# Relative attention in a six-layer decoder kernel: a finished batch's normalisation and store placed one step later, behind the step's writes to DRAM

## The chip, the cores and the metric

The kernel runs on one core of one Trainium2 chip. Five engines take part, each with an instruction stream of its own: PE (TensorE, matrix products), DVE (VectorE), ACT (ScalarE), POOL (GpSimd) and SP (SyncE, which here only issues DMAs). They meet through semaphores. The metric is the device time of one execution in microseconds, as the median of several runs; lower is better. The profile is one execution of its own, with its own time.

## The reference

The program is a decoder of two layers with three parts each. After each part comes a residual sum and a layer norm: `x = layernorm(x + part(x))`. The input x is 8 batches x 256 tokens x 256 channels in float32. The parts are retention, cross attention, channel mix, relative attention, an mLSTM cell and a product-key expert layer. The change touches only the fourth, relative attention (16 heads of 16 channels, distances clipped at 64):

```
dist  = clip(idx[None, :] - idx[:, None], -R, R) + R
score = einsum('bhqd,bhkd->bhqk', q, k) + einsum('bhqd,qkd->bhqk', q, rel_emb_k[dist])
attn  = softmax(score)
ctx   = einsum('bhqk,bhkd->bhqd', attn, v) + einsum('bhqk,qkd->bhqd', attn, rel_emb_v[dist])
x     = layernorm(x + ctx @ W_out + b_out)
```

The terms in `rel_emb_k[dist]` and `rel_emb_v[dist]` need each row of a 256 x 256 table shifted by its own row number.

## The kernel before, in words

The whole program is one launch. The six parts are software pipelines that overlap at their seams. Relative attention (`relative_attention_layer`) runs from about 615 us to about 1058 us of the span. Its first steps run beside the last of the channel mix, and from its step 18 on the opening of the mLSTM runs beside it.

The work is cut into units. A unit U is a group of four heads of one batch, so a batch b is units 4b to 4b+3 and there are 32 units. `STEPS` runs s from -5 to 38; in step s every engine handles several units at different stages: the table of query times distance embedding of unit s+3, the scores and exponentials of unit s+1, the turning of the probabilities of unit s, the turning of the skewed probabilities of unit s-2, the values of unit s-3. A finished batch b passes its last stages at fixed steps: PE gathers it at step 4b+7, turns it at 4b+8, and multiplies by the output weights at 4b+9. At step 4b+10 (`out_of(s - 1) == b`):

- DVE adds the residual into `yout` and takes mean and variance (L1670, L131 to L136), before the step's additions of bias (L1630);
- POOL raises the variance to -1/2 (L1532, `rel_rs`);
- DVE, later in the same step, behind its copy of the turned skewed probabilities (L1688) and before its copies of the step's table (L1697), waits for `rstd`, normalises `yout` in place (L141, two instructions) and counts up `y_ready`;
- SP waits for `y_ready`, stores `yout` to DRAM (L1474), and for b = 0 and 1 also loads the input of batch b+6 (L1306, through `take_x`).

The skewing goes through DRAM. SP's step, in its order, is: two loads that read the table back with a skewed pitch, the bias (L1458, after its save has landed); two skewed loads of the probabilities (L1470, after their save has landed); the store and input load above; the save of the table of unit s+3 (L1484, 1 MB, after ACT's and DVE's copies); the save of the probabilities of unit s+1 (L1491, 1 MB, after ACT's exponentials). Each engine takes its stream in order, and so does SP: an instruction that waits holds all behind it.

From step 21 to 28 the mLSTM's steps are chained behind these on two queues. On SP: a load of `mls_v_in` for value batch k+1 (L2032, 256 KB), a wait until POOL has centred batch k, and its store to `mls_v_rows` (L2046). On POOL, from step 20 on: wait for value batch k, then centre it (L2091 to L2099). POOL takes that work behind its own relative-attention step, so the `rel_rs` of the next step comes after it. At step 30 the mLSTM's loads of the finished batches 0 to 4 follow (L1886, each waiting until the batch is stored), and at step 31 the loads of the context, with that of batch 5 behind the first.

```
if (b := out_of(s - 1)) is not None:              # SP, between the loads and the saves
    sp.wait_ge(y_ready, b + 1)
    sp.dma_start(batch_of(x_out, b), yout[:, b % 2]).then_inc(stored[b % 2], 16)
    if b + XS < nb:
        sp.wait_ge(x_used, b + 1)
        take_x(sp, b + XS)
```

Of the kernel before, what the change touches and what calls it, by code (L numbers as in the profile page):

```python
# [51 lines left out]
def batch_of(ap, n):  # L52

    return ap[bass.ds(n, 1)].rearrange("a (t p) d -> p (a t) d", p=P)


def load_all(engine, sem, pairs):

    for to, what in pairs:
        engine.dma_start(to, what).then_inc(sem, 16)  # L60
    return 16 * len(pairs)
# [60 lines left out]
def place(h):  # L122

    g, r = h // 4, h % 4
    return g // 2, g % 2, ROWS * r
# [1205 lines left out]
def relative_attention_layer(nc, mem, bank, ident, room, yout, two_before, before, x_out, w, nb):  # L1331
# [4 lines left out]
    def sem(name):  # L1336
        return nc.alloc_semaphore("rel_" + name)
# [11 lines left out]
    XS = 6  # L1349
# [24 lines left out]
    x_loaded, stored = [sem(f"x_loaded{k}") for k in range(XS)], [sem(f"stored{k}") for k in range(2)]  # L1374
# [11 lines left out]
    x_used, var, rstd, y_ready = sem("x_used"), sem("var"), sem("rstd"), sem("y_ready")  # L1386
# [7 lines left out]
    def unit(k):  # L1394
        return k if 0 <= k < UNITS else None

    def batch(k):
        return k // GROUPS if k % GROUPS == 0 and 0 <= k // GROUPS < nb else None

    def scores_of(s):  # L1400
        return unit(s + 1)

    def table_of(s):
        return unit(s + 3)

    def turn_of(s):
        return unit(s)
# [10 lines left out]
    def project_of(s):  # L1418
        return batch(s + 4)
# [7 lines left out]
    def out_of(s):  # L1427
        return batch(s - 9)

    def head(U, r):  # L1430
        return (U // GROUPS,) + place(4 * (U % GROUPS) + r)

# [4 lines left out]
    def take_x(sp, b):  # L1437
        before["give_x"](sp, b, xin[:, b % XS], x_loaded[b % XS])

    def sync(sp):  # L1440
        load_all(sp, loaded, loads)
        sp.dma_start(wv[:], w["wv"]).then_inc(wv_loaded, 16)
        load_all(sp, late, late_loads)
        yield
        two_before["work_taken"](sp)
        take_x(sp, 0)
        yield
        for s in STEPS:
            if 1 <= s + 6 < XS:
                take_x(sp, s + 6)  # L1450
            if (U := unit(s + 2)) is not None:

                sp.wait_ge(qr_saved[U % 2], 16 * (U // 2 + 1))
                if U >= 2:
                    sp.wait_ge(summed_ready, 4 * (U - 1))
                for t, first in ((0, 2 * (P - 1)), (1, 2 * (2 * P + REACH - 2))):
                    skewed = bass.AP(qr_rows[U % 2].tensor, first, [[2 * PW - 2, P], [PW, 2], [1, 2 * NEAR]])
                    sp.dma_start(bias[:, U % 2, t, :, REACH * t:REACH * t + NEAR]  # L1458
                                 .rearrange("p h k e -> p h (k e)"), skewed).then_inc(bias_loaded[U % 2], 16)
            if (U := turn_of(s)) is not None:  # L1460
                if U == 0:
                    before["over"](sp)
                    before["kept"](sp)

                sp.wait_ge(p_saved[U % 2], 16 * (U // 2 + 1))
                if U >= 3:
                    sp.wait_ge(wT_mm, 2 * (U - 2))
                for t, first in ((0, 2 * NEAR), (1, 0)):
                    skewed = bass.AP(p_rows[U % 2].tensor, first, [[2 * PW + 2, P], [PW, 2], [1, 2 * NEAR]])
                    sp.dma_start(by_dist[:, U % 3, t, :, 0:NEAR].rearrange("p h k e -> p h (k e)"), skewed)\  # L1470
                        .then_inc(dist_loaded[U % 3], 16)
            if (b := out_of(s - 1)) is not None:
                sp.wait_ge(y_ready, b + 1)
                sp.dma_start(batch_of(x_out, b), yout[:, b % 2]).then_inc(stored[b % 2], 16)  # L1474
                if b + XS < nb:
                    sp.wait_ge(x_used, b + 1)
                    take_x(sp, b + XS)
            if (U := table_of(s)) is not None:

                sp.wait_ge(qr_act, 2 * (U + 1))  # L1480
                sp.wait_ge(qr_dve, 2 * (U + 1))
                if U >= 2:
                    sp.wait_ge(bias_loaded[U % 2], 32 * (U // 2))
                sp.dma_start(qr_rows[U % 2], qr[:, U % 2].rearrange("p h k e -> p h (k e)"))\  # L1484
                    .then_inc(qr_saved[U % 2], 16)
            if (U := scores_of(s)) is not None:

                sp.wait_ge(probs_ready, 4 * (U + 1))
                if U >= 2:
                    sp.wait_ge(dist_loaded[(U - 2) % 3], 32 * ((U - 2) // 3 + 1))  # L1490
                sp.dma_start(p_rows[U % 2], probs[:, U % 2, :, REACH:REACH + ROW]  # L1491
                             .rearrange("p h k e -> p h (k e)")).then_inc(p_saved[U % 2], 16)
            yield s


# [123 lines left out]
    def vector(dve):  # L1619
# [27 lines left out]
        for s in STEPS:  # L1647
            if (b := project_of(s - 1)) is not None:
                dve.wait_ge(v_mm, b + 1)
                if b >= 3:  # L1650
                    dve.wait_ge(values_mm, GROUPS * (b - 2))
                dve.tensor_copy(v[:, b % 3, :, :, 0:HD].rearrange("p t h e -> p (t h) e"),
                                bank[2][:].rearrange("p (a e) -> p a e", e=HD)).then_inc(v_ready, 1)
            if (b := gather_of(s - 1)) is not None:
                dve.wait_ge(oU_turned, b + 1)
                if b >= 2:
                    dve.wait_ge(o_turned, b - 1)
                for t in range(TT):
                    parts = bank[1 + t][:].rearrange("p (h e) -> p h e", e=VW)
                    dve.reciprocal(rsum[:, t], parts[:, :, HD])  # L1660
                    dve.drain()
                    last = dve.tensor_tensor(o[:, b % 2, t].rearrange("p (h e) -> p h e", e=HD),
                                             parts[:, :, 0:HD], over(rsum[:, t], HD), ALU.mult)
                last.then_inc(o_ready, 1)
            if (b := out_of(s - 1)) is not None:
                dve.wait_ge(o_mm, b + 1)
                dve.wait_ge(xbo_ready, b + 1)
                if b >= 2:
                    dve.wait_ge(stored[b % 2], 16 * (b // 2))
                dve.tensor_tensor(yout[:, b % 2], tiles(bank[0]), xin[:, b % XS], ALU.add).then_inc(x_used, 1)  # L1670
                dve.drain()
                row_stats(dve, yout[:, b % 2], st[:, b % 2], mv[:, b % 2], ve[:, b % 2]).then_inc(var, 1)
            if (U := turn_of(s - 1)) is not None:
                keep_turned(U, 3)
            if (U := scores_of(s)) is not None:
                add_bias(U, 0)
            if (U := turn_of(s)) is not None:
                keep_turned(U, 1)
            if (U := scores_of(s)) is not None:
                add_bias(U, 1)  # L1680
                add_bias(U, 2)
            if (U := scores_of(s)) is not None:
                add_bias(U, 3)
            if (U := dist_of(s)) is not None:
                dve.wait_ge(wT_mm, 2 * U + 1)
                if U >= 2:
                    dve.wait_ge(values_mm, U - 1)
                dve.tensor_copy(wT[:, U % 2, 0].rearrange("p r s -> p (r s)"), bank[6][:]).then_inc(wT_dve, 1)  # L1688
            if (b := out_of(s - 1)) is not None:
                dve.wait_ge(rstd, b + 1)  # L1690
                normalise(dve, yout[:, b % 2], yout[:, b % 2], mv[:, b % 2], rs[:, b % 2])[-1].then_inc(y_ready, 1)
            if (U := table_of(s)) is not None:
                if U >= 2:
                    dve.wait_ge(qr_saved[U % 2], 16 * (U // 2))
                for r in range(2, 4):
                    dve.wait_ge(qr_mm, 4 * U + r + 1)
                    dve.tensor_copy(table_cut(U, r), bank[r][:, 0:2 * BAND]  # L1697
                                    .rearrange("p (t k) -> p t k", t=TT)).then_inc(qr_dve, 1)
            if (U := unit(s - 1)) is not None:
                far_sums(U)  # L1700
            if x_turn_of(s) == 0:
                dve.wait_ge(late, 16 * len(late_loads))
                dve.wait_ge(const_mm, 1)
                dve.tensor_tensor(const_row[:], tiles(bank[3]), bo[:].unsqueeze(1).broadcast_to([P, TT, D]),
                                  ALU.add).then_inc(const_ready, 1)
            yield s
# [1638 lines left out]
```

## Time and profile before

| what | value |
|---|---|
| median of 3 runs | 1798.02 us (1796.23 to 1798.17) |
| profiled execution: its own time, span | 1808.23 us, 1806.5 us |
| PE busy, share of the span | 1618.8 us, 90% |
| DVE, ACT, POOL busy | 65%, 37%, 18% |
| mean granted TensorE clock | 0.946 |
| chain that ended last | PE 60%, issue 14%, DVE 10%, ACT 4%, DMA 4%, POOL 3% |
| DMA, whole span | 97 GB/s |
| DMA in relative attention | 328, 315, 321, 321, 336, 322, 331, 303 GB/s in 8 of 40 slices |

The page divides the span into 40 slices of about 45 us. In 32 of them the DMA engines are idle or lightly used; in those of relative attention they are 90% busy or more. "Idle before" names the time for which an engine had nothing to run ahead of an instruction and what ended it.

### The profile page before, as it was taken

The page shows a single profiled execution, that of the slowest core. Times are in us where ns is not written, and L with a number is a line of the kernel's source. Part 1 is how long each engine was busy: PE and PEld are TensorE (multiplying, and loading weights), DVE is VectorE, ACT ScalarE, POOL GpSimd, SP SyncE. Part 2 cuts the span into 40 slices and gives each one's busy share as a digit, 9 for nine tenths or more (in the row PEclk, how much of TensorE's full clock was granted, in tenths as well). Part 3 has the DMA queues.
Part 4 walks back from the last instruction along what each step waited for, and adds up shares of the span by engine and source line. Part 5 has one row for each costly group of instructions (what it writes and reads, how often), then busy time and mean ns, then how long its engine had stood idle before and what let it go on. Part 6 is the DMA issues. An engine that isn't in the chain of part 4 may idle for free.

```text
span 1806.5 us, 38627 instructions
## 1 busy us (share of the span) xinstructions
PE 1618.8 (90%) x14760; PEld 1267.3 (70%) x14760; DVE 1171.4 (65%) x3823; ACT 676.3 (37%) x1426; POOL 316.2 (18%) x335
## 2 busy tenths in 40 slices
PE   6799996899997879899978788997999999999997
PEld 4677775666665757677756657775887888788876
DVE  3555664455563756566656447449888889889884
ACT  3333331245556446565545444132222222222210
POOL 1443434200001200000122006410010001000100
PEclk9899998999999989999989887899999999999999
DMA  3100000000111279999999951320000000000000
GB/s 127 47 19 19 19 13 19 12 19 25 31 55 49 82 285 328 315 321 321 336 322 331 303 178 35 123 94 2 2 13 2 13 8 7 13 2 13 6 3 13
DMA packets 98358, 177.29 MB, mean 98 GB/s; under 512 B 16128, under 2 KB 82688, under 8 KB 93440
## 3 DMA queue, kind: packets, MB, share of 16 engines
q1 hardware_dynamic: 98176, 174.82, 28.1%
q8 instruction: 120, 1.97, 0.5%
q14 instruction: 62, 0.51, 0.1%
HBM read 92.88 MB, written 81.79 MB: 97 GB/s over the span
## 4 chain that ended last, share of the span: by engine, by line
PE 60%; issue 14%; DVE 10%; ACT 4%; DMA 4%; POOL 3%; DVEq 2%; POOLq 2%; SPq 0%; ACTq 0%
PE bank L104 20%; PE bank L2995 10%; PE bank L112 5%; PE bank L2955 3%; PE bank L2982 3%; DMA rel_p_rows<-rel_probs 2%; PE bank L970 2%; PE bank L1746 2%; PE bank L986 1%; PE bank L97 1%; ACT rel_probs L1547 1%; PE bank L1780 1%; PE bank L1002 1%; PE bank L1767 1%; DVE first_shared L422 1%
## 5 line engine op out<-in xcount | busy, mean ns | idle before, releaser
L104 PE MATMUL bank<-per_xT,per_down 128*128 128x256 f32 x1024 | 250.7, 390 | 2.3 <-ACT per_xT L2674 1.6
L2995 PE MATMUL bank<-per_up,per_act_w 128*128 128x256 f32 x1024 | 242.7, 383 | 0.0
L2995 PEld LDWEIGHTS bank<-per_up,per_act_w 128*128 128x128 f32 x1024 | 195.5, 192 | 27.0
L2681 ACT ACTIVATE per_act_w<-bank 128x512 f32<-128x512 f32 x128 | 76.3, 597 | 364.4 <-PE bank L104 329.8
L104 PEld LDWEIGHTS bank<-per_xT,per_down 128*128 128x128 f32 x1024 | 190.4, 192 | 29.9 <-issue 2.7
L1547 ACT ACTIVATE rel_probs<-later_shared,rel_low 128x256 f32<-128x256 f32 x256 | 114.9, 519 | 32.1 <-DVE rel_low L1630 32.1
L1630 DVE CUSTOM_DVE_ANT_0 later_shared<-bank,later_shared 128x256 f32<-128x256 f32 x256 | 92.9, 419 | 40.0 <-PE bank L1746 19.0
L922 DVE TENSOR_REDUCE xat_mx<-bank 128x2 f32<-128x512 f32 x128 | 79.4, 684 | 34.9 <-PE bank L970 34.9
L2661 POOL TENSOR_TENSOR per_sim<-per_sim,per_best_i 128x512 f32<-128x512 f32 x32 | 41.9, 1329 | 332.5 <-DVE per_sim L2799 332.5
L104 PE MATMUL bank<-ret_x2T,ret_w_in 128*128 128x256 f32 x384 | 93.0, 399 | 7.5 <-issue 7.5
L1780 PE MATMUL bank<-ident,rel_probs 128*128 128x128 f32 x512 | 88.0, 308 | 1.1 <-ACT rel_pT L1555 1.1
L104 PEld LDWEIGHTS bank<-ret_x2T,ret_w_in 128*128 128x128 f32 x384 | 74.8, 199 | 20.1 <-issue 8.9
L2849 DVE TENSOR_TENSOR per_hot_x<-per_picksT,per_iota_x 128x2048 f16<-128x2048 f16 x64 | 87.5, 1367 | 0.0
L2862 DVE TENSOR_TENSOR per_act_w<-bank,per_act_w 128x512 f32<-128x512 f32 x128 | 82.5, 686 | 7.7 <-PE bank L2982 2.6
L1780 PEld LDWEIGHTS bank<-ident,rel_probs 128*128 128x128 f32 x512 | 73.0, 209 | 19.6 <-issue 18.8
L2982 PEld LDWEIGHTS bank<-per_hot_y,per_hot_x 64*128 64x128 f16 x4096 | 55.7, 93 | 42.1 <-issue 39.7
L1555 ACT ACTIVATE rel_pT<-bank 128x512 f32<-128x512 f32 x64 | 38.3, 599 | 104.4 <-PE bank L1780 104.4
L1746 PE MATMUL bank<-later_shared 32*128 32x256 f32 x512 | 52.9, 417 | 26.5 <-DVE later_shared L1697 9.8
L2982 PE MATMUL bank<-per_hot_y,per_hot_x 64*128 64x32 f16 x4096 | 61.9, 173 | 15.6 <-DVE per_act_w L2862 15.6
L893 ACT ACTIVATE first_shared<-bank 128x512 f32<-128x512 f32 x128 | 66.2, 613 | 11.5 <-PE bank L986 11.5
L1767 PE MATMUL bank<-rel_band_k,later_shared 32*128 32x191 f32 x512 | 54.9, 375 | 11.2 <-DVE rel_low L1630 7.0
L422 DVE TENSOR_TENSOR first_shared<-bank,ret_seen 128x256 f32<-128x256 f32 x128 | 45.1, 413 | 30.2 <-PE bank L530 30.1
(365 smaller groups left out, 3171.3 us busy)
## 6 DMA issues: line engine op xcount, KB each, us to landing
rel_qr_rows<-later_shared SPq DMA_DIRECT2D x32, 1024.0 KB, 7.8
rel_p_rows<-rel_probs SPq DMA_DIRECT2D x32, 1024.0 KB, 9.8
later_shared<-rel_qr_rows SPq DMA_DIRECT2D x64, 384.0 KB, 4.7
rel_by_dist<-rel_p_rows SPq DMA_DIRECT2D x64, 384.0 KB, 5.2
per_down<-in_per_down SPq DMA_DIRECT2D x1, 4096.0 KB, 12.4
per_up<-in_per_up SPq DMA_DIRECT2D x1, 4096.0 KB, 13.3
ret_xin<-in_x SPq DMA_DIRECT2D x8, 256.0 KB, 2.9
xat_cT<-in_contextT SPq DMA_DIRECT2D x8, 256.0 KB, 3.0
```

The lines of the kernel that those rows point to most:

```text
L104: last = pe.matmul(dst, wt[:, c], src[:, c, :], start=c == 0, stop=c == DC - 1)
L112: last = pe.matmul(dst[:, t, :], src[:, c, t * P:t * P + P], wt[:, c, :], start=c == 0, stop=c == DC - 1)
L922: dve.tensor_reduce(mx[:, b % 2, :, 4 * (U % GROUPS) + r], tiles(first_bank(U, r)), AX.X, ALU.max).then_inc(max_taken, 1)
L1547: last = nc.scalar.activation(probs[:, U % 2, r // 2, at:at + SEQ, r % 2], summed[:, r, t], ACT.Exp, bias=low[:, r, t:t + 1], scale=-1.0)
L1630: last = dve.tensor_tensor_reduce(summed[:, r, t], tiles(bank[r])[:, t], bias[:, U % 2, t, r // 2, :, r % 2], 1.0, 3.0e38, ALU.add, ALU.mi ...
L1746: last = pe.matmul(tiles(bank[r])[:, t], qT[at:at + ROWS, b % 2, par, c, t * P:t * P + P], kT[at:at + ROWS, b % 2, c, :], start=True, stop ...
L1780: last = pe.transpose(bank[4 + r % 2][:, (2 * c + t) * P:(2 * c + t) * P + P], probs[:, U % 2, r // 2, at:at + P, r % 2], ident[:])
L2681: nc.scalar.activation(act_w[m % 2][:, 2 * k:2 * k + 2, :], tiles(bank[3 + k % 2]), ACT.Gelu_apprx_tanh).then_inc(gelu_ready, 1)
L2849: dve.tensor_tensor(fours(hot_x[:, slot]), four(0, wide_x), pattern(iota_x, wide_x), ALU.is_equal)
L2862: dve.tensor_tensor(of, bank[5 + par][:].rearrange("p (s j) -> p j s", j=COLS), of, ALU.mult)\
L2982: last = pe.matmul(bank[5 + par][:, s * COLS:s * COLS + COLS], hot_x[own, slot, s], hot_y[own, slot, k, s], start=k == 0, stop=k == 1)
L2995: last = pe.matmul(tiles(bank[7])[:, t, :], act_w[n % 2][:, k, t * P:t * P + P], up[:, k, :], start=k == 0, stop=k == COLS - 1)
```

## The change

Both places at which a finished batch is normalised (DVE) and stored (SP) now ask a new function `end_of(s)` in place of `out_of(s - 1)`. It gives batches 0 to 5 one step later, at step 4b+11, and leaves 6 and 7 at steps 34 and 38. On SP the block also moves inside the step, from before the two saves to behind them. The residual sum, the statistics and POOL's power stay at step 4b+10. The number of instructions and DMAs is the same.

```diff
+    def end_of(s):
+        last = out_of(s - 1)
+        return last if last is not None and last >= nb - 2 else out_of(s - 2) if out_of(s - 2) != nb - 2 else None
@@ sync, before the saves
-            if (b := out_of(s - 1)) is not None:
-                sp.wait_ge(y_ready, b + 1)
-                sp.dma_start(batch_of(x_out, b), yout[:, b % 2]).then_inc(stored[b % 2], 16)
-                if b + XS < nb:
-                    sp.wait_ge(x_used, b + 1)
-                    take_x(sp, b + XS)
@@ sync, behind the save of the probabilities
+            if (b := end_of(s)) is not None:
+                sp.wait_ge(y_ready, b + 1)
+                sp.dma_start(batch_of(x_out, b), yout[:, b % 2]).then_inc(stored[b % 2], 16)
+                if b + XS < nb:
+                    sp.wait_ge(x_used, b + 1)
+                    take_x(sp, b + XS)
@@ vector, same place in the step
-            if (b := out_of(s - 1)) is not None:
+            if (b := end_of(s)) is not None:
                 dve.wait_ge(rstd, b + 1)
                 normalise(dve, yout[:, b % 2], yout[:, b % 2], mv[:, b % 2], rs[:, b % 2])[-1].then_inc(y_ready, 1)
```

## Rows read from the trace of the kernel before

**Rows 1.** Waits of SP's queue: line, releaser, us in total, times, longest.
```profile
SPq L1458 <- DMA rel_qr_rows<-later_shared: 147.8, 29, 7.6
SPq L1474 <- DVE rel_yout L141: 23.1, 3, 11.4
```

**Rows 2.** Busy time by stretch; the last three columns: clock, DMA share, GB/s.
```profile
857.67:904.57 46.90, 42.66 (x401) 34.00 (x400) 29.70 (x106) 27.80 (x65) 6.35 (x15) 0.96 0.97 332
904.57:954.77 50.20, 38.96 (x341) 30.86 (x340) 26.34 (x91) 23.67 (x55) 12.35 (x26) 0.86 0.94 335
954.77:1007.02 52.25, 43.92 (x429) 34.24 (x429) 33.37 (x120) 30.01 (x69) 14.62 (x33) 0.90 0.92 326
```

**Rows 3.** The same view by step, cut at the start of SP's L1470.
```profile
821.63:834.37 12.74, 10.86 (x93) 8.35 (x86) 7.38 (x28) 6.80 (x16) 1.28 (x1) 0.87 0.98 337
...
916.53:931.36 14.83, 7.91 (x73) 6.00 (x74) 6.80 (x25) 3.64 (x10) 4.15 (x9) 0.65 0.73 252
931.36:943.80 12.44, 10.41 (x105) 7.97 (x105) 8.02 (x28) 6.69 (x16) 3.50 (x8) 0.86 1.03 367
943.80:954.77 10.97, 9.76 (x74) 8.19 (x67) 3.84 (x10) 6.10 (x14) 4.70 (x9) 1.00 1.03 385
954.77:967.43 12.66, 11.58 (x128) 9.14 (x131) 9.62 (x35) 7.42 (x18) 3.49 (x8) 1.00 0.85 305
967.43:982.89 15.46, 12.60 (x129) 9.47 (x117) 9.00 (x34) 8.34 (x21) 4.17 (x9) 0.78 0.87 305
982.89:995.46 12.57, 10.15 (x108) 8.19 (x108) 9.35 (x31) 7.77 (x20) 3.49 (x8) 1.00 1.02 360
```

**Rows 4.** Timeline of DVE: start, us, instruction, idle before and releaser.
```profile
922.52 0.74 DVE L141 TENSOR_SCALAR rel_yout<-rel_yout,rel_mv,rel_rs 128x256 f32<-128x256 f32 x2 [8.06 <-POOL rel_rs L1532]
...
973.38 0.73 DVE L141 TENSOR_SCALAR rel_yout<-rel_yout,rel_mv,rel_rs 128x256 f32<-128x256 f32 x2 [4.00 <-POOL rel_rs L1532]
```

**Rows 5.** Timeline of POOL around the powers of batches 3 and 4.
```profile
917.31 0.72 POOL L2091 TENSOR_TENSOR mls_v_sum<-mls_v_in 128x256 f32<-128x256 f32 x1 [29.94 <-DMA mls_v_in<-in_context]
...
921.76 0.72 POOL L1532 TENSOR_TENSOR rel_rs<-rel_ve,rel_half 128x2 f32<-128x2 f32 x1
...
972.61 0.73 POOL L1532 TENSOR_TENSOR rel_rs<-rel_ve,rel_half 128x2 f32<-128x2 f32 x1
```

**Rows 6.** Timeline of SP's queue in steps 21, 22 and 26.
```profile
906.61 1.44 SPq L2032 DMA_DIRECT2D mls_v_in<-in_context  x1
...
916.53 0.87 SPq L1470 DMA_DIRECT2D rel_by_dist<-rel_p_rows  x2
923.28 0.36 SPq L1474 DMA_DIRECT2D x_after_rel<-rel_yout  x1
924.24 0.33 SPq L1484 DMA_DIRECT2D rel_qr_rows<-later_shared  x1
...
967.43 0.88 SPq L1470 DMA_DIRECT2D rel_by_dist<-rel_p_rows  x2
974.14 0.36 SPq L1474 DMA_DIRECT2D x_after_rel<-rel_yout  x1
```

**Rows 7.** Timeline of SP's queue in step 10, a store without a stall.
```profile
775.24 0.46 SPq L1474 DMA_DIRECT2D x_after_rel<-rel_yout  x1
775.80 0.41 SPq L1306 DMA_DIRECT2D rel_xin<-x_after_mix  x1
```

**Rows 8.** Busy time by stretch of 2 us, columns as in rows 2.
```profile
922.00:924.00 2.00, 0.23 (x1) 0.23 (x2) 1.48 (x4) 0.00 (x0) 0.48 (x1) 0.50 0.00 0
```

**Rows 9.** The chain that ended last, at the stage's end: start, us, what.
```profile
1017.15 8.03 DMA rel_p_rows<-rel_probs
```

**Rows 10.** Timeline of SP's queue in step 31.
```profile
1027.13 4.03 SPq L2054 DMA_DIRECT2D later_shared<-in_contextT  x7
```

**Rows 11.** Timeline of PE: its first product with a context.
```profile
1043.88 1.08 PE L2306 MATMUL bank<-later_shared,mls_w_c 128*32 128x256 f32 x12
```

**Rows 12.** Landing of the eight stores of rel_yout, from the view of that tile.
```profile
DMA to landing us min/median/max: 2.1/4.3/6.2
```

## The prediction

> **What bounds the kernel now.** I read the page's slices first. They show relative attention as the one stage whose DMA engines are nearly full while PE is busy too. So I asked two things: how regular its steps are, and which queue waits for what.
>
> SP's own waits come next [rows 1]. The wait for the table's save to land, ahead of the bias loads, stands at 147.8 us over 29 times, 5.1 us each. SP's loop is save, land, load back, save again. The wait for a normalised batch is 23.1 us in only 3 times. A wait that is rare and long is a stall, not a rhythm.
>
> The stretches of four steps give the size of the irregularity [rows 2]: 46.90 us undisturbed, then 50.20 and 52.25 us in the two stretches where the mLSTM's values also pass. By step [rows 3], two intervals stand out, 14.83 and 15.46 us. The four others in which values pass take 12.44, 10.97, 12.66 and 12.57 us, mean 12.16. The two long ones are steps 22 and 26, where batches 3 and 4 finish.
>
> The timelines name the cause. In step 22 DVE sat idle 8.06 us before it normalised, released by POOL's power, and in step 26 4.00 us [rows 4]. POOL was late because its stream is in order. It waited until 917.31 for a value batch that SP had issued at 906.61 [rows 5, 6], centred it until 921.8, and only then took the power at 921.76. SP had finished its skewed loads at 917.40 and issued the store at 923.28 and the table's save at 924.24 [rows 6]: 5.9 us, and in step 26 from 968.31 to 974.14, 5.8 us. Behind DVE's normalisation stood its table copies, and behind those PE's next scores and SP's save. From 922 to 924 us the DMA share is 0.00, PE runs 0.23 us and the clock is at 0.50, its lower level of 1.2 GHz, after PE had stood idle [rows 8].
>
> **The change, part by part.** First, POOL's lateness. The power stays in step 22 and comes at 921.8 as before. The normalisation that needs it now runs in step 23, behind DVE's L1688 there. DVE began to wait for it at 922.52 - 8.06 = 914.5; one unstalled step of 12 us later is near 926, so the operand is 4 us early. In step 26 it is ready at 973.3 [rows 5] and wanted 12 us behind 973.38 - 4.00, near 981. So both idle times go. What is late next is the transfers. A step needs its two 1 MB saves and four loads, and the intervals with values run at a DMA share of 1.02 to 1.03 in three of those four [rows 3]. I therefore don't count the 12.06 us of idle DVE. I count what a step costs when nothing stalls, the mean 12.16: 14.83 - 12.16 = 2.7 us and 15.46 - 12.16 = 3.3 us, together 6.0 us.
>
> Bounds of this term. Below: let both long stretches reach only the share 0.97 of the undisturbed one [rows 2] with their transfers unchanged. That gives 50.20 x (1 - 0.94/0.97) = 1.6 and 52.25 x (1 - 0.92/0.97) = 2.7, so 4.3 us; as the transfers may stretch in time once they overlap more, I let the floor be 2. Above: the whole idle time of DVE, 12.1 us.
>
> The Trainium skill, page "DMA: Bandwidth & Descriptors", section "Specifications", gives a limit of about 358 GB/s for a core's share of HBM. An estimate by that page: the two stretches carry 335 x 50.20 = 16.8 MB and 326 x 52.25 = 17.0 MB, which at 358 GB/s take 47.0 and 47.6 us, so the gain could not pass 3.2 + 4.7 = 7.9 us. The trace goes past that limit, with 367 and 385 GB/s over whole steps, so it is no wall here.
>
> Second, SP's issues. In steps 10, 14, 18 the store sits between the skewed loads and the table's save: 0.56 us from its start to the next issue; with the 0.41 us of the input load for batches 0 and 1, 0.97 us [rows 7]. The save goes out that much earlier now, 0.97 + 0.97 + 0.56 = 2.5 us at most. The moved issues land in the 5.1 us wait for the table's save [rows 1], so they cost SP nothing; in steps 23 and 27 SP also waits there for POOL's centring, and the 0.56 us would come onto its path only if that wait used up all of the 5.1. But the step of batch 1 already has a DMA share of 0.98 at 12.74 us [rows 3]: the save would only queue earlier behind the skewed loads. I take 0.5 us, ends 0 and 2.5.
>
> Third, the transfers themselves. The store (256 KB) and the input load now stand ahead of the next step's bias loads and, in steps 23 and 27, of the value load. At 335 GB/s one such transfer takes 0.78 us. Six stores and two loads give at most 6.3 us if each delays the bias that DVE's additions then wait for. But the bytes stood ahead of the saves before and delayed the same bias through them, so what is new is only their place. I take a cost of 0.6 us, ends 0 and 6.3.
>
> Fourth, DVE's work. The normalisation takes 0.73 us [rows 4] ahead of the table copies, now in step 4b+11, which lacks the sum and the statistics. One step gains it, one loses it: 0, ends -0.7 x 6 and +0.7 x 6, so 4.4 us either way.
>
> Fifth, the end. In step 30 the store no longer precedes the last save of probabilities. That save is on the chain that ended last [rows 9], so its issue, 0.56 us [rows 7], comes off the path: 0.6 us, and up to 0.8 more for the 256 KB no longer ahead of it. In step 31 SP must now wait for batch 5's store to land before it issues the load of batch 5 and seven context loads. Those went out at 1027.13 for 4.03 us, and PE first used a context at 1043.88; that leaves 12.7 us for landing [rows 10, 11], while a store takes 2.1 to 6.2 us to land [rows 12]. I count 0; if the cover were gone, up to 4 us.
>
> Sum: 6.0 + 0.5 - 0.6 + 0 + 0.6 = 6.5 us. The profiled execution would take 1808.23 - 6.5 = 1801.7 us. It lies 10.2 us above the median of the runs, and I carry the difference over unchanged: 1798.02 - 6.5 = 1791.5 us.
>
> **The rivals.**
>
> *Transfer-bound.* The idle times vanish, but the stage is held by the DMA engines and most of it turns into longer landings. For it: shares of 0.92 to 0.97 in all three stretches [rows 2], and the interval behind the first stall at 1.03. Against it: the share of exactly 0 inside that stall [rows 8], time that no later step can use. It gives 2 to 4 us, around 1795.
>
> *Full return.* DVE, PE and POOL regain the whole idle time, 8.06 + 4.00 = 12.1 us, around 1786. For it: SP's save at step 22 could go out at 917.5 in place of 924.24, 6.7 us earlier, and PE no longer runs at the lower clock (0.65 mean in that interval). Against it: after the stall SP's loop caught up, since a stall of 5.9 us lengthened its interval by only 14.83 - 12.16 = 2.7 us [rows 3], so most of the 6.7 us had already been given back.
>
> *The displaced transfers (slower).* The store is now consumed ahead of the bias loads, and in steps 4b+12 DVE's additions wait for them. Place: the bias loads behind SP's L1458. Price: 6.3 us by the term above, against a stall term at its low end of 2 to 3 us, so 3 to 4 us slower, near 1801. It decides once more than 0.8 us of each of the eight transfers shows up on the chain. For it: the DMA engines are full in the steps behind a store, so a transfer placed ahead is waited for in full [rows 3]. Against it: the same bytes delayed the same loads before. The Trainium skill, page "DMA: Bandwidth & Descriptors", section "Queues, rings and completion order", says that each DMA engine consumes a queue's descriptors in ring order. By that rule a store issued behind the probabilities' save cannot delay that save, but does stand ahead of every bias load issued later. That the value load behind a save takes from 906.61 to about 917.3 to land [rows 5, 6] agrees.
>
> *Nothing moves.* The normalisation meets a POOL that is late by a full step as well. POOL frees itself at 921.8 each time, 4 us ahead; the values would have to land 4 us later than they do. It gives 1798.
>
> **How the numbers follow.** The forecast, a gain of 4.5 to 9 us, has 0.52. Transfer-bound has 0.24, full return 0.12, the displaced transfers 0.07, nothing moves 0.05. About 0.2%, 3.6 us, is what a measurement of this kernel can tell from no change. Faster by more than that: the forecast, full return and 0.11 of the transfer-bound case, 0.75. Within: the rest of that case, most of nothing moves, and 0.02 of displaced, 0.20. Slower: 0.05. The range 1785.5 to 1797.5 holds the forecast, the transfer-bound case and most of full return, and leaves out the slower case and no movement.
>
> **What would show it.** DVE's L141 no longer waits for POOL but for the last batch or two; SP's L1474 waits nearly nothing in steps 11 to 31; the intervals of steps 22 and 26 fall from 14.83 and 15.46 to about 12; the DMA share is nowhere 0 between 915 and 980; the clock stays up there. POOL's own times for the values shift with the steps. SP's L1886 shows a wait for batch 5's store of 2.1 to 6.2 us, with no wait of PE behind it. I am wrong if these intervals shrink and others grow by as much (transfer-bound), or if DVE's waits before L1630 for the bias grow in steps 4b+12 (displaced transfers).

## The result, and the profile after

The changed kernel takes 1784.0 us (median of 20 runs, 1776.35 to 1800.3), the kernel before 1798.1 us (20 runs). The ratio is 0.9909, 95% interval 0.9890 to 0.9929, so 16 us faster by the ratio and 14 by the medians. The forecast was a gain of 6.5 us and a range down to 1785.5; the gain was more than twice as large, and the time lies just below the range. The profiled execution of the changed kernel took 1785.93 us with a span of 1784.1.

In the changed kernel SP's L1463, L1475, L1483, L1490 and L1494 are the bias loads, the skewed probability loads, the table's save, the probabilities' save and the store. First SP's waits, as in [rows 1]: line, releaser, us in total, times, longest. The second row is the moved wait for the normalised batch.

```profile
SPq L1463 <- DMA rel_qr_rows<-later_shared: 141.2, 29, 7.1
...
SPq L1494 <- DVE rel_yout L141: 7.2, 1, 7.2
```

Three waits of 23.1 us in all became one of 7.2 us. The one left is the wait for the last batch, which was 11.4 us before; the waits of 5.9 and 5.8 us in steps 22 and 26 are gone. Next the busy time by stretch, in the columns of [rows 2]: the three stretches of four steps, then the intervals of steps 22 and 26 that answer to 14.83 and 15.46 us in [rows 3].

```profile
852.37:898.83 46.46, 42.27 (x419) 33.62 (x417) 31.11 (x110) 29.26 (x69) 6.36 (x15) 0.96 0.95 335
898.83:945.22 46.39, 42.13 (x400) 33.95 (x399) 29.93 (x105) 27.64 (x64) 12.40 (x26) 0.96 1.02 367
945.22:992.99 47.77, 41.33 (x392) 32.54 (x388) 31.30 (x111) 26.92 (x62) 14.69 (x33) 0.93 0.98 355
```
```profile
910.73:922.19 11.46, 10.61 (x97) 8.42 (x97) 7.53 (x28) 7.96 (x18) 4.19 (x9) 0.89 1.01 371
...
956.33:969.30 12.97, 11.06 (x115) 8.92 (x118) 10.42 (x34) 8.43 (x20) 4.19 (x9) 1.00 0.95 338
```

The stretches with values fell from 50.20 and 52.25 us to 46.39 and 47.77, and the same bytes now pass at 367 and 355 GB/s in place of 335 and 326. DVE's timeline, as in [rows 4], shows both normalisations without an idle time in brackets:

```profile
918.15 0.73 DVE L141 TENSOR_SCALAR rel_yout<-rel_yout,rel_mv,rel_rs 128x256 f32<-128x256 f32 x2
...
964.05 0.73 DVE L141 TENSOR_SCALAR rel_yout<-rel_yout,rel_mv,rel_rs 128x256 f32<-128x256 f32 x2
```

POOL is as late as before, as in [rows 5]. It still waits for the value batch and takes the power behind it, 5.2 us after the start of SP's step in both kernels. For batch 3 the power ends at 916.7, 1.5 us before DVE wants it. For batch 4, and for both in the second profile of this kernel, it is 1.8, 1.5 and 1.4 us.

```profile
911.47 0.73 POOL L2096 TENSOR_TENSOR mls_v_sum<-mls_v_in 128x256 f32<-128x256 f32 x1 [30.64 <-DMA mls_v_in<-in_context]
...
915.96 0.73 POOL L1537 TENSOR_TENSOR rel_rs<-rel_ve,rel_half 128x2 f32<-128x2 f32 x1
```

SP's queue in step 23 shows the new order: table, probabilities, store, value load.

```profile
922.19 0.87 SPq L1475 DMA_DIRECT2D rel_by_dist<-rel_p_rows  x2
923.17 0.41 SPq L1483 DMA_DIRECT2D rel_qr_rows<-later_shared  x1
923.68 0.52 SPq L1490 DMA_DIRECT2D rel_p_rows<-rel_probs  x1
924.25 1.16 SPq L1494 DMA_DIRECT2D x_after_rel<-rel_yout  x1
925.47 1.07 SPq L2037 DMA_DIRECT2D mls_v_in<-in_context  x1
```

At the stage's end, as in [rows 10, 11], SP waits for batch 5's store between the first context load and the seven others. PE reaches its first product with a context 15.5 us earlier than before.

```profile
1011.18 0.47 SPq L2059 DMA_DIRECT2D later_shared<-in_contextT  x1
1015.93 0.36 SPq L1891 DMA_DIRECT2D later_shared<-x_after_rel  x1
1016.34 3.54 SPq L2059 DMA_DIRECT2D later_shared<-in_contextT  x7
```
```profile
1028.36 1.08 PE L2311 MATMUL bank<-later_shared,mls_w_c 128*32 128x256 f32 x12
```

One view of the timed runs matters for what follows. The 20 executions of the changed kernel spread over 24 us, so I compare the stage itself. Its last store is issued at 1057.58 us before and at 1042.15 after, 15.4 us earlier. A single pair of profiles scatters too: in the second profile of each kernel, below, the two times are 1054.05 and 1043.47, 10.6 us apart. Counted from step 9 to step 31 the pairs give 16.0 and 14.0 us, mean 15.0.

### The profile page after: what moved, and what is told of

It is laid out like the page before. It is cut to its first block, busy times and chain, and to the rows that moved or that the text cites. A ratio compares the mean times of both kernels' runs of the same rounds, so it can differ in the third digit from the quotient of the medians.

```text
span 1784.1 us, 38627 instructions
## 1 busy us (share of the span) xinstructions
PE 1602.5 (90%) x14760; PEld 1255.9 (70%) x14760; DVE 1173.3 (66%) x3823; ACT 676.9 (38%) x1426; POOL 316.9 (18%) x335
## 4 chain that ended last, share of the span: by engine, by line
PE 62%; DVE 11%; issue 11%; ACT 5%; DMA 4%; POOL 3%; DVEq 2%; POOLq 1%; SPq 0%; ACTq 0%
PE bank L104 20%; PE bank L3000 10%; PE bank L112 5%; DMA rel_p_rows<-rel_probs 3%; PE bank L2960 3%; PE bank L2987 3%; ACT rel_probs L1552 2%; PE bank L1751 2%; PE bank L970 2%; PE bank L1785 2%; PE bank L986 2%; PE bank L97 2%; PE bank L1002 1%; DVE first_shared L422 1%; PE bank L1772 1%
## 5 line engine op out<-in xcount | busy, mean ns | idle before, releaser
L352 ACT ACTIVATE first_shared<-bank 128x128 f32<-128x128 f32 x128 | 35.3, 277 | 78.5 <-DVE first_shared L422 73.5
```

## The experiments

Each kernel's profile gives three times, cut at the start of SP's skewed probability loads: steps 9 to 21 (three stores, two input loads, no stall), steps 21 to 29 (batches 3 and 4, the values) and steps 29 to 31. The three stretches are in us. "Time" is the ratio to the kernel before, timed beside it, with its 95% interval.

| kernel | 9 to 21 | 21 to 29 | 29 to 31 | time |
|---|---|---|---|---|
| before | 142.32 | 102.45 | 18.17 | |
| before, again | 140.68 | 102.63 | 17.68 | 1.0014 (0.9984 to 1.0044) |
| order only | 135.16 | 102.27 | 16.69 | 0.9980 (0.9947 to 1.0012) |
| delay only | 142.26 | 92.69 | 16.14 | 0.9940 (0.9910 to 0.9970) |
| POOL's order only | 140.53 | 92.69 | 18.46 | 0.9948 (0.9916 to 0.9981) |
| order and POOL's order | 136.28 | 93.71 | 15.93 | 0.9943 (0.9918 to 0.9968) |
| after | 135.98 | 94.16 | 16.76 | 0.9909 (0.9890 to 0.9929) |
| after, again | 137.96 | 91.81 | 17.26 | 0.9922 (0.9891 to 0.9953) |
| after, store ahead | 137.88 | 93.99 | 16.54 | 0.9920 (0.9890 to 0.9950) |
| after, input load ahead | 138.52 | 91.73 | 17.07 | 0.9920 (0.9891 to 0.9950) |
| after, table's save first | 138.74 | 90.04 | 15.80 | 0.9906 (0.9869 to 0.9943) |
| after + 1 KB ahead x32 | 134.52 | 92.15 | 17.24 | 0.9899 (0.9867 to 0.9931) |
| after + 256 KB behind x32 | 140.48 | 95.66 | 17.84 | 0.9959 (0.9932 to 0.9987) |
| after + 256 KB ahead x32 | 142.58 | 96.78 | 18.05 | 1.0017 (0.9992 to 1.0043) |

**The order alone.** The block of SP moves behind the saves of the same step; DVE's part stays.

```diff
-            if (b := out_of(s - 1)) is not None:      # ahead of the saves
-                ... store, input load
+            if (b := out_of(s - 1)) is not None:      # behind them, same step
+                ... store, input load
```

> Half of the change: SP's store and input load stand behind the two saves of the same step 4b+10; nothing is delayed by a step, so DVE still waits for POOL's power in steps 22 and 26. Theory A (two causes: the stalls of DVE behind POOL give about 8 us, SP's issues and transfers ahead of the saves give the other 6 to 7): 5 to 7 us faster than before, all of it in steps 10 to 20, the idle times of 8 and 4 us of DVE still there. Theory B (the stalls are the whole cause, the 6 us in steps 9 to 21 between the two profiles are scatter): no change, within 2 us. Theory C (DVE's normalisation in the crowded step 4b+10 is what cost): within 2 us.

Measured: 1798.69 us against 1801.28, too little to be told from none. The profile is clearer. DVE's stalls are there in full:

```profile
913.68 0.73 DVE L141 TENSOR_SCALAR rel_yout<-rel_yout,rel_mv,rel_rs 128x256 f32<-128x256 f32 x2 [7.82 <-POOL rel_rs L1532]
...
964.26 0.74 DVE L141 TENSOR_SCALAR rel_yout<-rel_yout,rel_mv,rel_rs 128x256 f32<-128x256 f32 x2 [4.49 <-POOL rel_rs L1532]
```

Steps 21 to 29 take 102.27 us, as before, and steps 9 to 21 fall by 7 us. SP no longer waits for the normalised batch ahead of the saves, and the two long intervals are still 15.35 and 15.31 us: SP now waits for DVE's table copies instead (L1477, 18.0 us in five waits from 895 to 1010 us). So it is DVE's stall that costs here, not SP's wait for the store. Theory A gets its shape here; its size rests on the profiles, as the interval of the timed runs holds both no gain and the 7 us.

**The delay alone.** `end_of` in both places, SP's block back ahead of the saves.

```diff
-            ...                                        # behind the saves
+            if (b := end_of(s)) is not None:           # ahead of the saves
+                ... store, input load
             if (U := table_of(s)) is not None:
```

> The other half: normalisation and store one step later, but the store and the input load stand ahead of the saves as before. Theory A: 7 to 9 us faster than before, no idle time of DVE behind POOL, intervals of steps 10, 14, 18 as before. Theory B and C: the whole gain, 14 us.

Measured: 1790.35 us, ratio 0.9940, 11 us faster. Steps 21 to 29 fall to 92.69 us and steps 9 to 21 stay at 142.26. Theory A expected 7 to 9 us; B and C, 14. The interval of the timed runs, 5 to 16 us, holds both; the two stretches speak for A. One detail differs from what A expected: the long intervals did not stay in steps 10 and 14, they moved with the block to steps 11 and 15 (here by stretch, columns as in [rows 2]), at a granted clock of 1.00.

```profile
790.03:803.99 13.96, 11.97 (x109) 9.76 (x108) 7.68 (x27) 7.80 (x19) 0.00 (x0) 1.00 0.88 304
...
837.65:850.87 13.22, 11.24 (x106) 9.15 (x105) 7.67 (x27) 6.77 (x16) 0.14 (x1) 1.00 0.97 332
```

**POOL's order alone.** The kernel before, with the centring one step later, so that the power comes first.

```diff
-    gpsimd=range(FRONT_STEP - 13, FRONT_STEP - 12 + nb)
+    gpsimd=(FRONT_STEP - 13, *range(FRONT_STEP - 11, FRONT_STEP - 11 + nb))
```

> The kernel before with POOL's centring of the value batches one step later (steps 21 to 28), so that each power is taken ahead of the wait for values; no other change. Theory A: the stalls of DVE in steps 22 and 26 go, 7 to 9 us faster. Theory B: 14 us faster. Theory C: 7 us or less, as the normalisation stays in its step. If the value batches' own wait in SP grows, up to 2 us less.

Measured: 1790.47 us, ratio 0.9948, the delay's effect without any delay. POOL's timeline shows the power 5 us ahead of the value batch for which it had waited:

```profile
910.23 0.73 POOL L1532 TENSOR_TENSOR rel_rs<-rel_ve,rel_half 128x2 f32<-128x2 f32 x1 [23.76 <-DVE rel_ve L136]
...
915.36 0.91 POOL L2091 TENSOR_TENSOR mls_v_sum<-mls_v_in 128x256 f32<-128x256 f32 x1 [4.40 <-DMA mls_v_in<-in_context]
```

Steps 21 to 29 over the whole: 102.45 us before and 92.69 here. The normalisation stayed in its crowded step and this stretch gained as much as with the delay, so theory C is out for it: what the delay brings there is that POOL is no longer waited for. The timed runs alone (3 to 15 us faster) would not tell the theories apart.

```profile
904.57:1007.02 102.45, 82.88 (x768) 65.10 (x767) 59.71 (x211) 53.68 (x124) 26.97 (x59) 0.88 0.93 330
```
```profile
903.46:996.15 92.69, 80.43 (x785) 63.46 (x785) 60.53 (x214) 55.71 (x128) 27.38 (x59) 0.98 1.02 367
```

**The two kernels once more.**

> The changed kernel again, on the chip of the three others, so that they can be compared with it: 14 us faster than before by every theory. Its second profile shows how far step intervals scatter between executions: by theory A the stretch of steps 9 to 21 is again near 136 us (142.3 in the profile of before), by theory B it may be anything from 136 to 142.

> The kernel before once more, for a second profile of it: ratio 1 within its interval. If 142.3 us in steps 9 to 21 is a property of the kernel and not scatter, it comes again within 2 us; the intervals of steps 22 and 26 are again above 14 us.

Measured: 1789.2 us, ratio 0.9922, and 1805.74 us, ratio 1.0014. The stretch of steps 9 to 21 took 137.96 us in the changed kernel and 140.68 in the kernel before. So single profiles scatter by 2 us there, and theory B is not refuted by one pair but by eight profiles: the four with everything ahead of the saves (before, again, delay only, POOL's order) lie from 140.53 to 142.32, mean 141.45; the four with everything behind (order only, order and POOL's order, after, again) from 135.16 to 137.96, mean 136.35.

Most of that difference lies in the steps where SP has both a store and an input load ahead of the saves. Those are steps 10 and 14, or 11 and 15 with the delay: their eight intervals take 12.07 to 13.96 us, mean 12.99. Steps 10, 11, 14 and 15 of the four other profiles average 11.23. That is 1.75 us for each of the two steps, 3.5 of the 5.1 us. In steps 21 to 29, where two lone stores pass, the order changes nothing: without the stall they take 92.69, 92.69 and 93.99 us with the stores ahead, and 93.71, 94.16, 91.81 and 91.73 behind. PE's clock was lower on average with everything ahead (0.95 to 0.96 in steps 9 to 21, against 0.97 to 1.00), but it isn't the whole cause: the longest of the eight intervals, 13.96, 13.32 and 13.22 us, all ran at 1.00.

Steps 22 and 26 of the kernel before took 14.80 and 15.51 us this time:

```profile
913.55:928.35 14.80, 7.60 (x56) 5.39 (x56) 6.81 (x25) 2.46 (x6) 4.14 (x9) 0.54 0.74 256
964.12:979.63 15.51, 12.67 (x132) 9.38 (x120) 9.42 (x36) 8.94 (x22) 4.16 (x9) 0.89 0.88 305
```

**Order and POOL's order together.** Both edits above on the kernel before, no delay.

> The kernel before with store and input load behind the saves of the same step 4b+10, and with POOL's centring one step later so that the powers are early; the normalisation is not delayed. If the change is only these two things (no stall behind POOL, SP's issues off the loop), it equals the changed kernel: 12 to 16 us faster than before. If the delay by a step has a worth of its own (DVE's crowded step 4b+10), it stays 4 us or more behind the changed kernel.

Measured: 1791.65 us, ratio 0.9943, 10 us faster; the interval overlaps that of the changed kernel's second timing. In its profile steps 9 to 31 take 245.92 us, against 246.90 and 247.03 in the changed kernel's. By the profile the delay has no worth of its own. The times lean the other way: 10 us is less than the 12 to 16 expected of the two things together, and 4 and 6 us behind the changed kernel's two timings, which is where the expectation had put a worth of the delay. The intervals overlap, so this stays open.

**One more DMA per step, three ways.** In each of 32 steps: 1 KB ahead of the saves, 256 KB ahead, 256 KB behind.

```diff
+    def extra(sp, U):
+        sp.dma_start(extra_rows[U], wo[:]).then_inc(extra_done, 16)   # or wo[:, 0, 0:2]: 1 KB
```

> The changed kernel with one more DMA in each of 32 steps, of 1 KB (8 bytes from each of 128 partitions of a weight tile, to a DRAM scratch that nobody reads), issued where the store used to stand: between the skewed loads and the table's save. It costs SP's issue time and next to no transfer. Theory D (SP's loop of save, land, load back is the path of each step, so what stands ahead of the saves is paid in full): 32 x about 0.5 us of issue, so 12 to 20 us slower than the changed kernel, near 1800. Theory E (the DMA engines' backlog sets the step, and an issue is hidden behind the skewed loads' transfer): within 4 us of the changed kernel.

> The same extra DMA at the same place, with 256 KB, the size of a store. Theory D: issue and transfer are both paid, 32 x (0.5 + 0.8) = 42 us slower than the changed kernel. Theory E (only bytes count): 32 x 0.8 = 25 us.

> The same 256 KB in each of 32 steps, behind the two saves. Theory D: it runs in SP's wait for the table's save, but delays the bias loads queued behind it; 0 to 12 us slower than the changed kernel, 20 us or more better than with the same bytes ahead. Theory E: the place does not matter, 25 us slower as with the bytes ahead.

Measured: 1782.42, 1804.5 and 1793.13 us. The small DMA costs nothing that shows: theory D's first half falls. It is issued for 0.47 us in each step, and SP's wait for the table to land shrinks from 141.2 to 113.8 us over the 29 times:

```profile
805.50 0.87 SPq L1482 DMA_DIRECT2D rel_by_dist<-rel_p_rows  x2
806.42 0.47 SPq L1450 DMA_DIRECT2D rel_extra<-rel_wo  x1
```
```profile
SPq L1470 <- DMA rel_qr_rows<-later_shared: 113.8, 29, 6.2
```

The bytes do cost, and more in one place than in the other: (1804.5 - 1782.4) / 32 = 0.69 us for each 256 KB ahead of the saves, (1793.1 - 1782.4) / 32 = 0.33 us behind them. By the intervals of the ratios each of the two is known to about 0.24 us either way, and their difference to about 0.21. In the profiles the difference is smaller: steps 9 to 31, with 22 such DMAs, take 243.91, 257.41 and 253.98 us, so 0.61 and 0.46 us each. The 22 us for the bytes ahead fit theory E (25) and not D (42). The 11 us behind fit D (0 to 12) and not E (25). Theory E is wrong in that the place matters, D in that the issue does.

**Which of the two transfers.** The changed kernel with only the six stores, or only the two input loads, back ahead of the saves.

> The changed kernel with the six stores ahead of the saves (one step later, as in the delay-only kernel) and only the two input loads behind them. The delay-only kernel spent 142.3 us in steps 9 to 21, the changed kernel 136.0 and 138.0. Theory F (the input load, a read from DRAM in 1 KB pieces, is what costs ahead of the saves): about 137 us here. Theory G (the store, or its wait for the normalisation, costs): about 142 us. In median time either lies within 5 us of the changed kernel.

> The opposite split: the two input loads ahead of the saves, the six stores behind. Theory F: about 140 to 142 us in steps 9 to 21, the long intervals being steps 11 and 15. Theory G: about 137 us.

Measured: 137.88 and 138.52 us in steps 9 to 21, 1.5 and 2.2 us above the mean of 136.35. With the loads ahead, steps 11 and 15 take 12.17 and 12.34 us, where the changed kernel's two profiles have 11.26 and 11.91, 10.94 and 10.78; but steps 12 and 16, which have no such load, are as long (12.11 and 12.23). With the stores ahead, steps 11 and 15 take 11.68 and 11.46 us. Its long intervals, 12.80 us in step 14 and 12.60 in step 19, aren't the stores' work: the changed kernel's first profile has 12.30 and 12.66 there. Neither F nor G holds alone, and the scatter of 2 us does not carry a finer split.

**The table's save first.** The changed kernel with L1483 ahead of the skewed probability loads.

> The changed kernel with the table's save issued ahead of the two skewed loads of the probabilities, so that its landing, for which SP waits 5 us a step, starts earlier. If the loop of table save and bias load bounds the step: up to 1 us a step, 10 to 25 us faster than the changed kernel. If the save must wait for DVE's table copies there (they end about when the skewed loads are issued now) or the bytes are the bound: no change, or up to 10 us slower as the skewed loads land later.

Measured: 1785.73 us, ratio 0.9906, not told from the changed kernel. Single steps now range from 9.5 to 14.8 us in a pattern of four, and the sum is much the same: 244.58 us in steps 9 to 31, against 246.90 and 247.03. The second expectation is what the trace shows. SP's wait for the table to land fell from 141.2 to 46.0 us, and in its place SP waits for DVE's table copies ahead of the save, 108.1 us in 29 times where it was 18.2 in nine:

```profile
SPq L1470 <- DVE later_shared L1702: 108.1, 29, 9.4
SPq L1463 <- DMA rel_qr_rows<-later_shared: 46.0, 24, 4.3
```

SP's loop alone does not set the stage's time.

## Why the prediction was wrong, point by point

The mechanism of the stall was right. POOL's power was what DVE, PE and SP waited for in steps 22 and 26, the delay removed it, and DVE's waits for POOL fell from 13.7 us in four times to 1.6 us in two, the last two batches. The margin was thinner than forecast: the operand came 1.4 to 1.8 us early, not 4 and nearly 8, as DVE came to it sooner than I took. The sizes were off in three terms, and the largest miss, 5.2 of 9.6 us, is that of the order.

**The stall term, 6.0 us, was 9.5.** Three profiles with the stall spend 102.45, 102.63 and 102.27 us in steps 21 to 29. Seven without it spend 91.7 to 94.2, mean 93.0. The step that failed is "I count what a step costs when nothing stalls, the mean 12.16", and it failed twice. The four intervals behind that mean stood beside the stalls and were no undisturbed steps: without stalls the eight intervals average 93.0 / 8 = 11.6 us. So the two long intervals fell from 30.4 us together to 23.4, by 7.1 where 6.0 was counted. And only these two were counted. The six others, at nothing in the sum, shrank from 72.0 to 69.6 us, 2.4 us. The bounds, 2 to 12.1, held the value.

**The order's terms, 0.5 - 0.6 = -0.1 us, were +5.1** in steps 9 to 21 (141.45 - 136.35). I looked for the gain in SP's issues and for a cost in the bytes. It is the other way round: an issue ahead of the saves costs nothing that shows (the 1 KB DMA), and bytes ahead of the saves cost 0.69 us per 256 KB where behind them they cost 0.33. My bound of 2.5 us for this term was a bound of issue time alone and was exceeded. "What is new is only their place" was the failing sentence: the place was the effect, and it was a gain, not a cost. Five transfers at 0.69 - 0.33 = 0.36 us explain 1.8 of the 5.1 us. The rest I can't assign to a cause; by place, 3.5 of the 5.1 us lie in the two steps with a store and a load together.

**The end, 0.6 us, was 1.5**: 18.1 us in steps 29 to 31 with the store ahead of the last save (three profiles), 16.6 without (seven). The size is that of the 0.6 us and the extra 0.8 together, but no run here parts the issue from the bytes.

The three add up to 9.5 + 5.1 + 1.5 = 16.1 us, against 15.0 in steps 9 to 31 by the two pairs of profiles of before and after, 15.4 and 10.6 by the stage's last store, and 16 and 14 by the two ratios.

**The terms at nothing.** DVE's normalisation in another step: POOL's order alone left it in place and steps 21 to 29 gained as much, so 0 holds by the profiles; the timed runs leave a few us open. SP's wait in step 31: it came, 4.3 us at the longest, and PE's first context product moved by the full 15.5 us, so it was covered.

**The rivals.** Transfer-bound fell: it took shares of 0.92 to 0.97 for nearly full, but the same bytes went from 330 to 361 GB/s in steps 21 to 29 once nothing stalled. The page of the Trainium skill "DMA: Bandwidth & Descriptors", section "Specifications", gives a limit of about 358 GB/s, and by the estimate worked out from it the gain in steps 21 to 29 could not pass 7.9 us; the trace runs at 361 to 370 GB/s over 92 us, and the gain was 9.5. Displaced transfers fell with its sign: the bytes cost less at their new place. Its mark did show a little: DVE's waits for the bias went from 4.3 us in two to 6.9 us in three, the longest, 3.58 us, in step 28 behind batch 4's store. But the kernel before waits 2.27 us in that step, and POOL's order alone, with the stores still ahead, 4.45 us. Full return, at 12.1 us, was nearest in size, but by luck: of DVE's idle 12.1 us 9.5 came back, and 6.6 us came from elsewhere. That the DMA share would be nowhere 0 between 915 and 980 us came true. I was also wrong that the granted clock would stay up between 915 and 980: in the changed kernel too it falls to the lower level, 1.2 GHz, for a while, here with PE busy 1.74 and 1.41 of the 2 us in the two stretches before.

```profile
918.00:920.00 2.00, 1.41 (x15) 1.00 (x12) 2.00 (x6) 2.00 (x6) 0.00 (x0) 0.94 0.99 404
920.00:922.00 2.00, 2.00 (x10) 2.00 (x11) 0.46 (x2) 1.26 (x3) 0.00 (x0) 0.50 1.03 373
```

**What stays open.** Why a store or input load costs about 1 us more ahead of the saves than behind (5.1 us for five) where 256 KB from a weight tile cost 0.36 more, and why lone stores in steps 21 to 29 show none of it. Their shorter pieces in DRAM are one possibility that was not tried. That a store and a load in one step cost more than each alone is another; the 1.5 and 2.2 us with either alone, with a scatter of 2 us, can't decide it. Also why the intervals beside the stalls were longer: step 23 took 13.07 us at a granted clock of 1.00 with the order alone, so PE's lower clock isn't needed for it, but no run shows what is. And whether the one-step delay is worth a few us beyond POOL's order, which the timed runs allow and the profiles don't show.

## What to carry to other kernels

When the intervals next to a stall serve as the measure of an undisturbed step, the stall comes out too small; take the measure from a stretch far from it, and count what its neighbours lose too. Where a queue's loop is save, land, load back, order its DMAs by what somebody waits for: here bytes that nobody waited for were cheaper behind the awaited save, while an issue of half a microsecond ahead of it was absorbed by the wait. An in-order engine that waits for one pipeline's data and then serves another's small operand (here 0.7 us of POOL) is worth looking for: here moving either the consumer or the other work by one step cured it.

## What was not expected of the hardware

A DMA busy share of 0.93 over the stage was no sign that the engines were full: 0.93 at 330 GB/s and 1.02 at 367 GB/s are the same bytes in 102.45 and 92.69 us. The average hid the stalls, and the share itself goes above 1.

The changed kernel's two profiled executions differ mostly outside the changed stage. They spend 246.90 and 247.03 us in steps 9 to 31. From the stage's last store to the end, the first two rows below are those executions and the third is that of the kernel with the input loads ahead. The longer the time, the lower the granted clock, 0.96, 0.94 and 0.97, while the instructions are all but the same in number.

```profile
1042.15:1784.10 741.95, 698.76 (x7198) 568.39 (x7194) 582.30 (x2142) 190.09 (x317) 105.34 (x102) 0.96 0.08 29
```
```profile
1043.47:1795.20 751.73, 712.18 (x7198) 579.35 (x7198) 580.63 (x2142) 190.42 (x317) 105.05 (x102) 0.94 0.08 28
```
```profile
1038.66:1776.40 737.74, 693.91 (x7198) 564.74 (x7196) 582.28 (x2142) 190.34 (x317) 105.55 (x102) 0.97 0.08 29
```
